# Fewer tokens computed directly: two Strassen groups of 768 tokens take the place of 512 direct tokens and one group of 1024

## Chip, core and metric

One core of one Trainium2 chip. The metric is the device time of one execution in microseconds; lower is better.

## What is computed

```python
# x: (16, 256, 512) f32; cond: (16, 256); W2, weight, rram_variation: (512, 512)
q_emb = relu(cond @ W3 + b3)                         # (16, 512)
h = relu(((256 * x + sum_tokens(x)) * q_emb) @ W2 + b2)
h_q = where(h > 0.33, 0.5, 0)                        # h is never below -0.33
w_q = where(w > 0.2, 0.6, where(w < -0.2, -0.6, 0)) + rram_variation
out = x + einsum('bsd,od->bso', h_q, w_q)
```

There are 4096 tokens (16 batches of 256) of 512 columns. The two big products are the hidden product (tokens by W2, in f32) and the output product (thresholded hidden values by w_q, in f32r with the weight split in a low and a high part).

## The kernel before

Everything lies in SBUF with the features on the partitions: each batch of x is loaded (SP queue), transposed in 32x32 blocks by VectorE (`transpose_batch`, L521 to 534), summed over its tokens (on VectorE for the batches of `VECTOR_SUMS`, by `prepare`, L576 to 583; on ScalarE for the others, by `accumulate`, L433), and scaled in place by ScalarE in four chunks (`scale`, L424 to 431, semaphore `s_xs`).

**Hidden product.** The first 1024 tokens (batches 0 to 3) are multiplied directly: 4 row blocks by 4 column blocks of 128 (L1003 to 1023), and VectorE thresholds the eight banks (`quantize`, L585 to 589). The other 3072 tokens are three groups of 1024. A group is one level of Strassen (Winograd's form): its first half of 512 tokens against its second half, 7 products `p1` to `p7` for each of two output blocks j, each product 2 matmuls of 512 columns; an f32 matmul shows as 2 instructions in the trace, so a product is 4 instructions and a group 56. VectorE makes four token sums for a group (`token_sum_1` to `_4`, L591 to 620, f32, both inputs in SBUF), and for each j it evicts with `c11`, `sum_16`, `sum_167`, `c22`, `c21`, `c12` (L623 to 665). ScalarE copies p1 (`copy_p1`, L452). POOL makes the sums of W2 (`s_mix`) once.

**Output product.** The 8 tiles of 128 tokens that were computed directly are projected directly (`project`, 8 matmuls of 512 columns each) into the banks out_ps; VectorE adds the residual (`finish`, L667). The tiles of the groups are projected in pairs, again by Strassen (`project_pair`, 28 matmuls of 256 columns for two tiles), with hidden sums by POOL and the last pair of tiles done directly. The weight's path: VectorE compares (L748, L750), POOL subtracts and adds rram (L322, L327, 4 instructions each), VectorE transposes (`transpose_weight`, L726), ScalarE rounds to the high part (L479), POOL subtracts the low part (L331). `project(0)` waits for the second low part (`s_wlo`).

**Order.** Each engine's order is written out by hand (VectorE L732 to 824, ScalarE L460 to 518, POOL L306 to 414, TensorE L1003 to 1072, SP L249 to 294). On TensorE: direct products, the 14 products of group 1 with `project(0..3)` put before the last one (L1037 to 1042), `project(4..7)`, then group 2, the four pairs of group 1, group 3, the four pairs of group 2 and the last pairs. The residual tiles lie in the eight slots of x_res: SP loads 8 tiles at once after the weight has been transposed, which lies in the same buffer before (L276 to 284), and loads the next 8 when the stores of the first 8 have landed.

Of the kernel before, what the change touches and what calls it, by code (L numbers as in the profile page):

```python
# [5 lines left out]
def adaln_ffn_kernel(  # L6
# [71 lines left out]
    GROUPS = B // 4  # L78
    LAST = GROUPS - 1

    PAIRS_OF = (0, 4, 4, 3)
# [4 lines left out]
    VECTOR_SUMS = (2, 3, 6, 7)  # L86

    XS_DONE = tuple((n + 1) * KD for n in range(B))
# [3 lines left out]
    with ctx:  # L92
# [34 lines left out]
        th_col = sbuf("th_col", [P, KD])  # L127
        warm = sbuf("warm", [P, D], mybir.dt.bfloat16)
# [10 lines left out]
        res = (x_res, x_res, x_res, x_res_last)  # L139
# [15 lines left out]
        s_x_res = [sem(f"x_res_loaded{g}") for g in range(GROUPS)]  # L155
        s_stored = [sem(f"stored{g}") for g in range(GROUPS)]
# [22 lines left out]
        s_th = sem("threshold_ready")  # L179
        s_mix_done = sem("weight_sum_ready")  # L180
# [47 lines left out]
        def _(sp):  # L228
# [4 lines left out]
            def load_res(g):  # L233
                sp.dma_start(res[g][:], x_tiles[:, g * TILES:(g + 1) * TILES]).then_inc(s_x_res[g], DMA)

            def store(g, tiles):
                for n, c in enumerate(tiles):
                    sp.wait_ge(s_out, (TILES if g == LAST else 0) + n + 1)
                    sp.dma_start(out_tiles[g * TILES + c], res[g][:, c]).then_inc(s_stored[g], DMA)

            def store_pairs(g):
                for c in range(PAIRS_OF[g]):
                    u = 4 * (g - 1) + c
                    sp.wait_ge(s_r12, u + 1)
                    sp.dma_start(out_tiles[g * TILES + c], res[g][:, c]).then_inc(s_stored[g], DMA)
                    sp.wait_ge(s_r2, 2 * (u + 1))
                    sp.dma_start(out_tiles[g * TILES + 4 + c], res[g][:, 4 + c]).then_inc(s_stored[g], DMA)
# [34 lines left out]
            store(0, range(TILES))  # L282
            sp.wait_ge(s_stored[0], DMA * TILES)
            load_res(1)
            sp.wait_ge(s_tr, B - 1)
            load_res(3)
            store_pairs(1)
            sp.wait_ge(s_stored[1], DMA * TILES)
            load_res(2)
            store_pairs(2)  # L290
            store_pairs(3)
            store(3, (3,))
            sp.wait_ge(s_stored[2], DMA * TILES)
            sp.wait_ge(s_stored[LAST], DMA * (TILES + 1))

        @block.gpsimd
        def _(pool):
# [50 lines left out]
            def hidden_sums(g):  # L348
                h = hid[:, g % 2].bitcast(F32)
                a11, a12, a21, a22 = h[:, 0:2, 0:TOK], h[:, 2:4, 0:TOK], h[:, 0:2, TOK:], h[:, 2:4, TOK:]  # L350
                sums = a_sum[:].bitcast(F32)
# [4 lines left out]
                if g > 1:  # L356

                    pool.wait_ge(s_pp[7], 4 * (g - 1))
                nc.gpsimd.tensor_tensor(a_sum[:, 0], a21, a22, ALU.add).then_inc(s_asum, 1)  # L359
                pool.wait_ge(s_asum, 4 * (g - 1) + 1)  # L360
                nc.gpsimd.tensor_tensor(a_sum[:, 1], sums[:, 0], a11, ALU.subtract).then_inc(s_asum, 1)
                nc.gpsimd.tensor_tensor(a_sum[:, 2], a11, a21, ALU.subtract).then_inc(s_asum, 1)
                pool.wait_ge(s_asum, 4 * (g - 1) + 2)
                nc.gpsimd.tensor_tensor(a_sum[:, 3], a12, sums[:, 1], ALU.subtract).then_inc(s_asum, 1)

            def add_pieces(g, c):
                u = 4 * (g - 1) + c
# [7 lines left out]
                for cols in COLS:  # L375
                    nc.gpsimd.tensor_tensor(res[g][:, 4 + c, cols], res[g][:, 4 + c, cols], pieces[:, 2, u % 2],  # L376
                                            ALU.add).then_inc(s_r2, 1)

            def last_hidden_sums(c):

                h = hid[:, LAST % 2].bitcast(F32)
                first, second = slice(c * P, (c + 1) * P), slice(TOK + c * P, TOK + (c + 1) * P)
                a11, a12, a21, a22 = h[:, 0:2, first], h[:, 2:4, first], h[:, 0:2, second], h[:, 2:4, second]
                sums = a_sum[:].bitcast(F32)
                done = 4 * (LAST - 1 + c)
                if c == 0:
# [710 lines left out]
```

## Time and profile before

| | |
|---|---|
| median of 3 runs | 173.6 us (173.01 to 173.63) |
| the profiled execution | 172.84 us, its span 170.9 us |
| TensorE, VectorE, ScalarE, POOL busy | 165.6, 131.4, 67.4, 85.4 us |
| granted TensorE clock | 1.000 (all 40 slices at 9) |
| data moved | 28.99 MB, mean 170 GB/s |

The profiled execution is 0.76 us below the median. 1.94 us of it lie outside the span. A row of the timeline gives start, duration, engine, line, operation and what was written from what; consecutive instructions of an engine overlap by some tens of ns, so the distance between two starts is less than the duration. A row of the chain gives the start and the length of a piece of the chain of work that ended last.

### The profile page before, as it was taken

The numbers are of one execution on the slowest core, as the hardware profiler recorded it, in microseconds if no ns is written. First come the engines' busy times: TensorE is split into PE (matmuls) and PEld (weight loads), VectorE is DVE, ScalarE is ACT, GpSimd is POOL, SyncE is SP. The second block draws the span as 40 slices with busy tenths as digits, with TensorE's granted clock in tenths as the row PEclk, the third lists the DMA queues.
The fourth block names the chain that finished last, engine by engine and source line by source line (L and its number), as shares of the span: only waits on it lengthen the run. The fifth ranks groups of instructions, "written<-read, shape, count | busy, mean of one in ns | idle before, by whom it ended". The sixth has DMA issues, their size and how long they took to land.

```text
span 170.9 us, 2183 instructions
## 1 busy us (share of the span) xinstructions
PE 165.6 (97%) x684; PEld 122.1 (71%) x684; DVE 131.4 (77%) x196; ACT 67.4 (39%) x173; POOL 85.4 (50%) x85
## 2 busy tenths in 40 slices
PE   7989999999999999999999999999999999999991
PEld 2889987777554578686653459997653559999991
DVE  3589998998998999774968998778736267776751
ACT  2155269936102259999007996432000001001000
POOL 3001950849105592560089302759099203999990
PEclk9999999999999999999999999999999999999999
DMA  5999999999600494729949005983293000353166
GB/s 164 255 245 234 228 214 227 222 216 219 121 0 0 118 358 120 140 64 260 398 120 372 16 0 154 342 308 124 94 341 117 0 4 6 118 195 117 70 251 232
DMA packets 31211, 28.99 MB, mean 170 GB/s; under 512 B 1600, under 2 KB 22368, under 8 KB 31200
## 3 DMA queue, kind: packets, MB, share of 16 engines
q1 hardware_dynamic: 30128, 28.07, 60.4%
q10 hardware_dynamic: 1008, 0.79, 1.5%
q8 instruction: 5, 0.08, 0.2%
q14 instruction: 6, 0.05, 0.1%
q0 software_dynamic: 64, 0.00, 0.0%
HBM read 20.47 MB, written 8.39 MB: 169 GB/s over the span
## 4 chain that ended last, share of the span: by engine, by line
PE 87%; DVE 4%; issue 2%; ACT 0%; DVEq 0%; ACTq 0%
PE out_ps L957 12%; PE hid_ps L957 10%; PE out_ps L934 9%; PE out_ps L1020 8%; PE hid_ps L866 6%; PE hid_ps L859 6%; PE hid_ps L927 6%; PE hid_ps L908 5%; PE hid_ps L920 5%; PE hid_ps L883 5%; PE hid_ps L900 5%; PE hid_ps L1007 5%; PE hid_ps L1012 4%; PE hid_ps L934 2%; DVE xT L532 1%
## 5 line engine op out<-in xcount | busy, mean ns | idle before, releaser
L430 ACT ACTIVATE xT<-xT,coef,q_scale 128x256 f32<-128x256 f32 x64 | 33.9, 592 | 13.2 <-DVE coef L583 7.3
L532 DVE STREAM_TRANSPOSE xT<-x_in 128x1024 f32<-128x1024 f32 x15 | 30.7, 2053 | 0.0
L436 ACT ACTIVATE junk<-xT,q_emb 128x256 bf16<-128x256 f32 x40 | 19.8, 496 | 13.5 <-DVE xT L532 13.4
L370 POOL TENSOR_TENSOR x_res<-x_res,pieces 128x256 f32<-128x256 f32 x8 | 5.9, 734 | 24.2 <-DVE x_res L706 24.2
L486 ACT ACTIVATE pieces<-out_ps 128x256 f32<-128x256 f32 x6 | 2.3, 383 | 31.8 <-PE out_ps L957 29.8
L1020 PE MATMUL out_ps<-xT,w_sb 128*128 128x512 f32 x32 | 14.1, 599 | 0.0
L376 POOL TENSOR_TENSOR x_res<-x_res,pieces 128x256 f32<-128x256 f32 x16 | 13.4, 862 | 0.0
L934 PE MATMUL out_ps<-wT_lo,hid 128*128 128x512 f32 x32 | 13.3, 415 | 0.0
L1020 PEld LDWEIGHTS out_ps<-xT,w_sb 128*128 128x128 f32 x32 | 9.8, 309 | 3.8 <-ACT xT L430 0.2
L934 PE MATMUL out_ps<-wT_hi,hid 128*128 128x512 f32 x32 | 12.5, 390 | 0.0
L359 POOL TENSOR_TENSOR a_sum<-hid 128x1024 fp32r<-128x1024 f32 x2 | 4.7, 2348 | 14.6 <-DVE t_sum L611 14.6
L927 PE MATMUL hid_ps<-xT,s_mix 128*128 128x512 f32 x24 | 11.8, 614 | 0.1
L920 PE MATMUL hid_ps<-t_sum,w_sb 128*128 128x512 f32 x24 | 11.3, 592 | 0.0
L908 PE MATMUL hid_ps<-t_sum,s_mix 128*128 128x512 f32 x24 | 11.3, 592 | 0.0
L883 PE MATMUL hid_ps<-t_sum,s_mix 128*128 128x512 f32 x24 | 11.3, 592 | 0.0
L900 PE MATMUL hid_ps<-t_sum,s_mix 128*128 128x512 f32 x24 | 11.3, 592 | 0.0
L866 PE MATMUL hid_ps<-xT,w_sb 128*128 128x512 f32 x24 | 11.0, 601 | 0.0
L859 PE MATMUL hid_ps<-xT,w_sb 128*128 128x512 f32 x24 | 10.9, 597 | 0.0
L331 POOL TENSOR_TENSOR wT_lo<-wT,wT_hi 128x1024 fp32r<-128x1024 f32 x2 | 4.7, 2366 | 11.9 <-ACT wT_hi L479 11.9
L920 PEld LDWEIGHTS hid_ps<-t_sum,w_sb 128*128 128x128 f32 x24 | 7.4, 308 | 3.6 <-issue 1.4
L866 PEld LDWEIGHTS hid_ps<-xT,w_sb 128*128 128x128 f32 x24 | 7.3, 309 | 3.3 <-ACT e L458 0.6
L643 DVE SCALAR_TENSOR_TENSOR e<-hid_ps,th_col,e 128x512 f32<-128x512 f32 x6 | 4.4, 740 | 6.7 <-PE hid_ps L908 6.7
(134 smaller groups left out, 410.6 us busy)
## 6 DMA issues: line engine op xcount, KB each, us to landing
x_in<-in_x SPq DMA_DIRECT2D x24, 256.0 KB, 5.6
x_res<-in_x SPq DMA_DIRECT2D x3, 2048.0 KB, 9.2
out<-x_res SPq DMA_DIRECT2D x24, 256.0 KB, 3.5
x_in<-in_x SPq DMA_DIRECT2D x1, 2048.0 KB, 9.4
out<-x_in SPq DMA_DIRECT2D x7, 256.0 KB, 2.1
x_in<-in_x SPq DMA_DIRECT2D x12, 128.0 KB, 6.2
w_sb<-in_L_cond_W SPq DMA_DIRECT2D x4, 256.0 KB, 6.0
x_res<-in_L_ffn_weight SPq DMA_DIRECT2D x4, 256.0 KB, 7.1
```

The costliest lines, as they stand in the source:

```text
L430: nc.scalar.activation(part, part, ACT.Identity, bias=coef[:, n, k:k + 1], scale=q_scale[:, n, k:k + 1]).then_inc(s_xs, 1)
L532: nc.vector.transpose(xT[:, s, :, cols].rearrange("p j (n t) -> p n j t", t=BLK), x_in[:, p % SLOTS, b * NB:(b + 1) * NB].rearrange("p n ( ...
L859: mm = nc.tensor.matmul(hid_ps[j][:], weight_block(0, 0, j, k), xT[:, g % 2, k, 0:TOK], start=(k == 0), stop=(k == 1))
L866: mm = nc.tensor.matmul(hid_ps[j][:], weight_block(0, 1, j, k), xT[:, g % 2, 2 + k, 0:TOK], start=False, stop=(k == 1), skip_group_check=True)
L883: mm = nc.tensor.matmul(hid_ps[2 - j][:], s_mix[:, 1, j, k], t_sum[:, 1, k], start=(k == 0), stop=(k == 1))
L900: mm = nc.tensor.matmul(hid_ps[3 - j][:], s_mix[:, 0, j, k], t_sum[:, 0, k], start=(k == 0), stop=(k == 1))
L908: mm = nc.tensor.matmul(hid_ps[2 - j][:], s_mix[:, 2, j, k], t_sum[:, 2, k], start=False, stop=(k == 1), skip_group_check=True)
L920: mm = nc.tensor.matmul(hid_ps[0][:], weight_block(1, 1, j, k), t_sum[:, 3, k], start=(k == 0), stop=(k == 1))
L927: mm = nc.tensor.matmul(hid_ps[3 - j][:], s_mix[:, 3, j, k], xT[:, g % 2, 2 + k, TOK:], start=False, stop=(k == 1), skip_group_check=True)
L934: mm = nc.tensor.matmul(bank[:, cols], hid[:, g % 2, k, c * P:(c + 1) * P], w[:, k, cols], start=(k == 0 and w is wT_lo), stop=(k == KD - ...
L957: mm = nc.tensor.matmul(pair_ps[bank][u % 2], hidden[:, k, tokens], w[:, k], start=(start and k == 0 and i == 0), stop=(stop and k == 1 an ...
L1020: mm = nc.tensor.matmul(out_ps[m][:], chunk_columns(w2_sb[:, k], m), xT[:, 0, k, TOK:], start=(k == 0), stop=(k == KD - 1))
```

## The change

- Direct: 512 tokens instead of 1024. Four groups: 768 tokens (batches 2 to 4), 768 (batches 5 to 7), 1024 and 1024. In the 768 groups a half is 384 tokens, so every matmul, eviction and token sum of theirs is 384 or 2x384 wide. xT and hid become rings of 2048 tokens; the same batches lie where they did.
- The four direct banks are thresholded by ScalarE, Sign and then Relu, instead of eight on VectorE. A column of biases (`bias_col`) is added on VectorE.
- Batch 4 is summed by VectorE (`prepare`), batch 6 by ScalarE; before it was the other way round.
- The hidden values of group 1 (tiles 4 to 9) are projected directly too, so that there are ten direct tiles and ten pairs in place of eight and eleven (`PAIRS_OF`). The pair's banks are taken by a written table (`SIDE`, `AHEAD`) as their number is odd.
- Group 1 uses the banks out_ps, group 2 the banks hid_ps.
- Tiles 8 and 9 use slots 0 and 1 of x_res: SP stores tiles 0 and 1, waits for them to land, and loads the residual of 8 and 9 (0.5 MB); the six tiles of group 2 are loaded after tiles 2 to 7 have landed.
- VectorE's two comparisons of the weight stand behind group 1's first evictions, `w_gt` after `c11(1, 1)` and `w_in` after `transpose_batch(6)`.

```diff
-    PAIRS_OF = (0, 4, 4, 3)
+    FIRST = (0, 512, 1280, 2048, 3072)
+    SIZE = (512, 768, 768, 1024, 1024)
+    HALVES = tuple(n // 2 for n in SIZE)
+    LAST_BATCH = tuple((f + n) // N - 1 for f, n in zip(FIRST, SIZE))
+    HALF_BATCH = tuple((f + n // 2 - 1) // N for f, n in zip(FIRST, SIZE))
+    DIRECT = 10
+    PAIRS_OF = {2: 3, 3: 4, 4: 3}
+    SIDE = (0, 1, 0, 0, 1, 0, 1, 0, 1, 0)
+    AHEAD = (None, None, 0, 2, 1, 3, 4, 5, 6, 7)
...
-    VECTOR_SUMS = (2, 3, 6, 7)
+    VECTOR_SUMS = (2, 3, 4, 7)
...
+        def hidden_bank(g, b):
+            return (out_ps if g == 1 else hid_ps)[b][:, 0:HALVES[g]]
...
@@ SP, behind load_pair(7)
-            store(0, range(TILES))
-            sp.wait_ge(s_stored[0], DMA * TILES)
+            store_direct((0, 1))
+            wait_stored(0)
             load_res(1)
+            store_direct(range(2, DIRECT))
+            wait_stored(1)
+            load_res(2)
...
@@ ScalarE
+            def quantize(m):
+                act.wait_ge(s_cls, m + 1)
...
+                nc.scalar.activation(sign[:], hid_ps[m][:], ACT.Sign, bias=bias_col[:, m:m + 1]).then_inc(s_sign, 1)
+                act.wait_ge(s_sign, m + 1)
+                nc.scalar.activation(hid[:, m, 0:TOK], sign[:], ACT.Relu).then_inc(s_cls_hid, 1)
...
             scale_summed(3)
-            sum_and_scale(4)
+            copy_p1(1, 0)
+            copy_p1(1, 1)
+            scale_summed(4)
             sum_and_scale(5)
-            scale_summed(6)
-            copy_p1(1, 0)
-            act.wait_ge(s_coef, len(VECTOR_SUMS))
-            scale(7, (0, 1))
-            copy_p1(1, 1)
-            scale(7, (2, 3))
+            for m in range(KD):
+                quantize(m)
+            sum_and_scale(6)
+            copy_p1(2, 0)
+            copy_p1(2, 1)
+            scale_summed(7)
...
@@ VectorE
             def token_sum_1(g):
+                dve.wait_ge(s_xs, KD * LAST_BATCH[g] + 2)
...
             def finish(c):
-                dve.wait_ge(s_x_res[0], DMA)
+                dve.wait_ge(s_x_res[0 if c < TILES else 1], DMA)
...
             prepare(3)
-            transpose_batch(4)
+            prepare(4)
             transpose_batch(5)
+            token_sum_1(1)
+            token_sum_2(1)
+            dve.wait_ge(s_th, 2)
+            c11(1, 0)
+            token_sum_4(1)
+            token_sum_3(1)
+            sum_16(1, 0)
+            c11(1, 1)
             dve.wait_ge(s_w, QUADS * DMA)
             nc.vector.tensor_scalar(w_gt, ...)
+            sum_167(1, 0)
+            c22(1, 0)
+            c21(1, 0)
+            sum_16(1, 1)
+            transpose_batch(6)
             dve.wait_ge(s_wq, 1)
             nc.vector.tensor_scalar(w_in, ...)
-            for m in range(KD):
-                quantize(0, m)
-            prepare(6)
+            sum_167(1, 1)
+            c22(1, 1)
+            c21(1, 1)
             prepare(7)
-            quantize(1, 0)
...
+            c12(1, 0)
+            c12(1, 1)
+            token_sum_1(2)
+            c11(2, 0)
+            token_sum_2(2)
+            token_sum_4(2)
+            c11(2, 1)
+            token_sum_3(2)
+            sum_16(2, 0)
+            transpose_weight(0)
+            sum_167(2, 0)
+            c22(2, 0)
+            c21(2, 0)
+            transpose_weight(1)
+            sum_16(2, 1)
+            c12(2, 0)
+            transpose_batch(8)
+            sum_167(2, 1)
+            c22(2, 1)
+            c21(2, 1)
             transpose_batch(9)
             finish(0)
             finish(1)
             finish(2)
             transpose_batch(10)
             finish(3)
-            c12(1, 1)
+            c12(2, 1)
             finish(4)
             transpose_batch(11)
-            for c in range(5, TILES):
+            for c in range(5, DIRECT):
                 finish(c)
...
@@ TensorE
+            products(1)
+            p3(1, 1)
+            products(2)
+            for t in range(4):
+                project(t)
+            p3(2, 1)
+            for t in range(4, DIRECT):
+                project(t)
+            for g in (3, 4):
+                products(g)
                 p3(g, 1)
-                for c in range(4):
+                for c in range(PAIRS_OF[g - 1]):
                     project_pair(g - 1, c)
```

`products(g)` is the old order p1 p1 p2 p2 p5 p6 p4 p7 p6 p3 p5 p7 p4. Group 1's `p1` waits for batch 2 and two chunks of batch 3, `p5` for `token_sum_1(1)`, which waits for two chunks of batch 4.

## Rows read from the trace of the kernel before

**Rows 1.** Busy time of each engine, share of the span, instructions (the page).

```profile
PE 165.6 (97%) x684; PEld 122.1 (71%) x684; DVE 131.4 (77%) x196; ACT 67.4 (39%) x173; POOL 85.4 (50%) x85
```

**Rows 2.** The chain that ended last, in order of time: start us, us, what.

```profile
17.01 7.47 PE hid_ps L1012 x32
24.47 14.03 PE out_ps L1020 x32
...
61.01 7.27 PE out_ps L934 x32
68.27 1.72 PE hid_ps L927 x4
...
77.30 3.43 PE hid_ps L859 x8
...
105.50 3.36 PE hid_ps L957 x28
```

**Rows 3.** Timeline of VectorE: start us, us, engine, line, operation, out<-in.

```profile
20.06 2.09 DVE L532 STREAM_TRANSPOSE xT<-x_in 128x1024 f32<-128x1024 f32 x1
...
23.61 4.02 DVE L532 STREAM_TRANSPOSE xT<-x_in 128x1024 f32<-128x1024 f32 x2
...
29.45 1.23 DVE L750 TENSOR_SCALAR x_res<-x_res 128x2048 f32<-128x2048 f32 x1
...
44.90 1.21 DVE L604 TENSOR_TENSOR t_sum<-xT,t_sum 128x1024 f32<-128x1024 f32 x1
46.14 1.23 DVE L619 TENSOR_TENSOR t_sum<-xT,t_sum 128x1024 f32<-128x1024 f32 x1
...
49.08 0.75 DVE L637 SCALAR_TENSOR_TENSOR n<-hid_ps,th_col,e 128x512 f32<-128x512 f32 x1
49.74 2.02 DVE L729 STREAM_TRANSPOSE wT<-x_res 128x1024 f32<-128x1024 f32 x1
52.27 0.75 DVE L643 SCALAR_TENSOR_TENSOR e<-hid_ps,th_col,e 128x512 f32<-128x512 f32 x1 [0.51 <-PE hid_ps L908]
53.13 0.69 DVE L650 TENSOR_TENSOR hid<-hid_ps,e 128x512 fp32r<-128x512 f32 x1
53.73 0.68 DVE L657 TENSOR_TENSOR hid<-hid_ps,e 128x512 fp32r<-128x512 f32 x1
```

**Rows 4.** Timeline of ScalarE.

```profile
3.12 1.28 ACT L422 ACT_TABLE_LOAD   x1 [3.12 <-issue]
...
27.84 2.08 ACT L430 ACTIVATE xT<-xT,coef,q_scale 128x256 f32<-128x256 f32 x4
...
31.92 2.08 ACT L430 ACTIVATE xT<-xT,coef,q_scale 128x256 f32<-128x256 f32 x4
...
40.25 0.60 ACT L458 ACTIVATE e<-hid_ps 128x512 f32<-128x512 f32 x1 [1.38 <-PE hid_ps L859]
...
56.40 1.04 ACT L479 CAST wT_hi<-wT 128x1024 fp32r<-128x1024 f32 x1 [3.56 <-DVE wT L729]
```

**Rows 5.** Timeline of POOL.

```profile
38.27 4.96 POOL L327 TENSOR_TENSOR x_res<-x_res 128x512 f32<-128x512 f32 x4 [2.54 <-DMA x_res<-in_L_ffn_rram_variation]
...
57.52 2.36 POOL L331 TENSOR_TENSOR wT_lo<-wT,wT_hi 128x1024 fp32r<-128x1024 f32 x1 [2.24 <-ACT wT_hi L479]
```

**Rows 6.** Timeline of VectorE around 41 us.

```profile
40.02 0.77 DVE L583 TENSOR_TENSOR coef<-x_sum,q_emb 128x4 f32<-128x4 f32 x1
...
41.95 2.37 DVE L596 TENSOR_TENSOR t_sum<-xT 128x1024 f32<-128x1024 f32 x1 [0.50 <-ACT xT L430]
```

**Rows 7.** SP's load of the last pair of batches; landing of L239's stores from 77.3.

```profile
74.62 2.63 SPq L231 DMA_DIRECT2D x_in<-in_x  x4
...
DMA to landing us min/median/max: 4.6/4.7/4.8
```

**Rows 8.** DMA issues by kind, KB each, median us to landing (the page).

```profile
x_res<-in_x SPq DMA_DIRECT2D x3, 2048.0 KB, 9.2
...
out<-x_in SPq DMA_DIRECT2D x7, 256.0 KB, 2.1
```

More of the change, by code:

```diff
@@ L154, in adaln_ffn_kernel @@
         s_x_in = [sem(f"x_in_loaded{p}") for p in range(PAIRS)]
-        s_x_res = [sem(f"x_res_loaded{g}") for g in range(GROUPS)]
-        s_stored = [sem(f"stored{g}") for g in range(GROUPS)]
+        RES_TILES = ((0, 8), (8, 10), (10, 16), (16, 24), (24, 32))
+        s_x_res = [sem(f"x_res_loaded{i}") for i in range(len(RES_TILES))]
+        STORES = ((0, 2), (2, 8), (8, 10), (10, 16), (16, 24), (24, 32))
+        s_stored = [sem(f"stored{i}") for i in range(len(STORES))]
         s_cond = sem("cond_loaded")
@@ L231, in load_pair, with load_res, store, store_direct @@
                     sp.dma_start(x_in[q * BLK:(q + 1) * BLK, p % SLOTS], x_split[p, q]).then_inc(s_x_in[p], DMA)
[L233 to L239, printed above, removed]
+            def load_res(i):
+                first, end = RES_TILES[i]
+                place = x_res_last if first >= 24 else x_res
+                sp.dma_start(place[:, first % TILES:first % TILES + end - first], x_tiles[:, first:end]
+                             ).then_inc(s_x_res[i], DMA)
+            def store(t):
+                n = [first <= t < end for first, end in STORES].index(True)
+                sp.dma_start(out_tiles[t], res(t)).then_inc(s_stored[n], DMA)
+            def store_direct(tiles):
+                for t in tiles:
+                    sp.wait_ge(s_out, t + 1)
+                    store(t)
+            def wait_stored(n):
+                first, end = STORES[n]
+                sp.wait_ge(s_stored[n], DMA * (end - first))
             def store_pairs(g):
                 for c in range(PAIRS_OF[g]):
-                    u = 4 * (g - 1) + c
+                    u = FIRST_PAIR[g] + c
                     sp.wait_ge(s_r12, u + 1)
-                    sp.dma_start(out_tiles[g * TILES + c], res[g][:, c]).then_inc(s_stored[g], DMA)
+                    store(FIRST_TILE[g] + c)
                     sp.wait_ge(s_r2, 2 * (u + 1))
-                    sp.dma_start(out_tiles[g * TILES + 4 + c], res[g][:, 4 + c]).then_inc(s_stored[g], DMA)
+                    store(FIRST_TILE[g] + HALVES[g] // P + c)
             sp.dma_start(cond_in[:], cond_rows).then_inc(s_cond, DMA)
@@ L769, in _ @@
             c21(1, 0)
-            transpose_weight(1)
             sum_16(1, 1)
-            for m in range(1, KD):
-                quantize(1, m)
-            c12(1, 0)
-            transpose_batch(8)
+            transpose_batch(6)
+            dve.wait_ge(s_wq, 1)
+            nc.vector.tensor_scalar(w_in, w_in, -TH_W, SC_W, ALU.is_lt, ALU.mult).then_inc(s_wq, 1)
             sum_167(1, 1)
@@ L803, in _ @@
                 if g < LAST:
[L804 removed]
+                    transpose_batch(13)
                 c21(g, 0)
@@ L962, in project_pair @@
             def project_pair(g, c):
-                u = 4 * (g - 1) + c
-                first, second = slice(c * P, (c + 1) * P), slice(TOK + c * P, TOK + (c + 1) * P)
-                summed = 4 * (g - 1 + (c if g == LAST else 0))
-                h = hid[:, g % 2]
+                u = FIRST_PAIR[g] + c
+                tile = FIRST_TILE[g] + c
+                first, second = tile_columns(tile), tile_columns(tile + HALVES[g] // P)
+                of_sum = slice(c * P, (c + 1) * P)
+                summed = 4 * (g - 2 + (c if g == LAST else 0))
+                h = hid[:]
                 top, bottom = slice(0, 2), slice(2, 4)
```

431 lines of the change are left out of this document (202 added, 229 removed).

## The prediction

> **What bounds the kernel now.** I read the busy line first. TensorE is busy 165.6 us, 97% of the span, VectorE 77% [rows 1]. Then the chain of waits in order of time: from 9 us on it is TensorE almost alone, direct products to 38.5 us, group 1 to 61.0, projections to 77.3, and so on [rows 2]. So TensorE's own work sets the end, and a change that shortens it pays in full, as long as its inputs keep up. Third, the timeline of VectorE: between 12 and 58 us it has almost no pause either [rows 3]. In that stretch there are two engines without slack, and this is where the change is made. I call T0 the moment when TensorE starts the first direct tile's projection, 61.01 us before [rows 2], and work out T0 first, then what follows it.
>
> **TensorE's work.** The 1024-wide group costs 56 instructions; the second direct half shows the price of one, 14.03 / 32 = 0.438 with its pauses, and a product of four instructions takes 1.72, so 0.43 each [rows 2]. Removed: the second half of the direct product, 14.0 us. The group of 1024 becomes 768: 56 instructions of 384 columns at 0.32 (three quarters of 0.43), 18.0 instead of 24.0. Added: a second such group. Up to T0 (one product of the last group stands behind it) TensorE did 61.0 - 24.5 = 36.5 us of work after the first direct half; now it has 108 instructions of 0.32, 34.8 us. That is 1.7 less. A 256-wide f32 instruction costs 7.47 / 32 = 0.233 where half of 0.43 is 0.215, so up to 0.02 of each may not shrink with the columns: 108 x 0.02 = 2 us at worst, nothing at best. I take nothing, as 384 is wide enough to cover the weight load like 512 (no row shows it), and keep 2 as a bound. After T0: the postponed p3 is 0.43 shorter, two more direct tiles cost 7.27 / 4 x 2 = 3.63, and a pair less saves 3.36 [rows 2]. Together -0.2. If TensorE never waited, the change would be worth 1.9 us.
>
> **VectorE's work up to T0.** T0 needs the low part of the second weight half: the second weight transpose, ScalarE's rounding (1.04) and POOL's subtraction (2.36), with the semaphores 3.6 us from the end of that transpose [rows 3 to 5]. VectorE stands at 23.7 us when batch 3 is prepared, as before (23.61, plus the new column of biases). Its list from there to the end of the second weight transpose, by distances between starts [rows 3]: batches 4 and 7 prepared, 23.61 - 20.06 = 3.55 each, 7.1; batches 5 and 6 transposed, 4.0; the weight's two transposes, 4.0; two comparisons of 1.2, 2.4; eight token sums. One of 1024 elements takes 1.24, and a quarter less columns takes off 0.31 at most; I take 0.95, so 7.6. Four c11 and three sum_16: 0.66 at 512 wide, less 0.13 (a quarter of the columns would be 0.16), 3.7. Three times sum_167, c22, c21: 0.86 + 0.60 + 0.60 at 512, 1.66 at 384, 5.0. Two c12, 0.9. The sum is 34.7 us, so the second weight transpose ends at 58.4 at the earliest and T0 is 62.0 at the earliest, where TensorE's own work would allow 59.3. The eight quantize operations that go to ScalarE take 5.4 us off VectorE, but a further group's sums and evictions cost more. So already without a single pause the 1.7 us of TensorE are not gained but turned into waiting, and 1.0 us is lost.
>
> **VectorE's pauses.** I go through the new order. (a) `token_sum_1(1)` waits for two chunks of batch 4. TensorE starts group 1 at about 24.9, as ScalarE scales batch 3 only then; the two copies of p1, 0.5 each (0.60 at 512 wide [rows 4]), stand ahead of batch 4, which is scaled from 28.4; VectorE waits 0.3. (b) sum_167 and c21 wait for TensorE, 0.2. (c) A comparison moves: POOL's eight weight operations start when `w_in` has been compared, before at 29.45 + 1.23 = 30.7 [rows 3], now at 41.6. Four of them take 4.96 [rows 5], so they run to 51.5, and that is when VectorE makes the coefficients of batch 7 and the token sums of group 2. The rows show what that costs: the coefficients of batch 7 took 0.77 for 4 columns, up to the end of one POOL operation, and the token sum that followed took 2.37 instead of 1.22, up to the end of POOL's row and 1.09 more [rows 5, 6]. Both have two inputs in SBUF; evictions from PSUM beside POOL keep their length. I book 0.85 for the coefficients (46.8 to 47.8), 1.2 for `token_sum_1(2)` and 0.4 for `token_sum_2(2)`. Between nothing (they meet gaps) and 3.3 (each meets a whole operation of 1.24) I take 2.45, nearest to the row. (d) `token_sum_1(2)` waits for ScalarE to scale half of batch 7, 0.3. Together 3.2: T0 = 62.0 + 3.2 = 65.2, 4.2 later than before. TensorE stands idle meanwhile ahead of p5(2,0), p3(2,0) and p7(2,1).
>
> **ScalarE.** A summed and scaled batch takes 31.92 - 27.84 = 4.1 [rows 4]. Batch 5 is done at 34.4, then four times Sign and Relu of 512 columns, 1.3 a pair by the 0.60 row, end at 39.7. Batch 6 is transposed at 40.35, so they cost nothing; only 0.7 us of cover is left, and anything beyond that delays p1(2,0). The one function table load in the trace takes 1.28 [rows 4]. By the Trainium skill (ScalarE: Activation LUTs, section "Table sets: the hidden batching unit") cheap functions such as relu, copy and identity are in every set; Sign is not in that list, and a switch costs 2.7 us by that page. By it the sum would hold if Sign is in the loaded set, and be an estimated 2 us larger (2.7 less the cover) if it isn't. No row shows which.
>
> **After T0.** The new residual slots. SP sends the loads of batches 14 and 15 when batch 11 is transposed, before at 74.62, T0 + 13.6 [rows 7]; now T0 + 13.2 as the p3 between is shorter. It takes 2.65, then tiles 0 and 1 are stored, the second 0.5 later, and such a store lands after 4.7 [rows 7]: T0 + 21.0. The load of tiles 8 and 9 follows. 2 MB land in 9.2 and a store of 256 KB in 2.1 [rows 8], so about 1.0 for each further 256 KB and 3.1 for this one: T0 + 24.2; nearest row above: 4.7. `finish(8)` waits for it and VectorE's whole queue behind it: two finishes 1.3, four token sums 4.9, two c11 1.3, sum_16(3,0) 0.75 [rows 3]. p7(3,0) is released at T0 + 32.5. TensorE would come to it at T0 + 19.5 (ten tiles 18.2, p3 1.3) + 7 products of 1.72 = T0 + 31.5. Loss 1.0, and 0.15 for the weight load that can't run ahead: 1.2, between 0 (the load lands a microsecond sooner) and 2.8. Groups 3 and 4 and their pairs are as before. POOL's hidden sums and pieces are the same per pair, and smaller in group 2.
>
> **The sum.** +4.2 (T0) - 0.2 + 1.2 = +5.2 on the profiled 172.84, so 178.0; the median of the runs stands 0.76 above that execution, so 178.8.
>
> **Rivals.**
> 1. The same place, less of it: POOL and VectorE meet in gaps and the residual comes in time. For it: POOL leaves a gap between operations into which the coefficients slipped. Then T0 = 62.7 to 63.4 and the result is 175.1 to 177.0.
> 2. TensorE stays the only bound: -1.9, 171.7 us, faster. It is one mechanism: the weight's second transpose would have to end at 55.7, 2.7 us ahead of VectorE's list, so the 384-wide operations and sums (28 of them) would have to be 0.1 us cheaper each than I take them, and no lock-out may occur. For it: TensorE's 97%. Against it: the rows give 34.7 us of list for 32 us of time, and before there is hardly any pause in it to use up.
> 3. The bare list: no pauses, residual in time. T0 = 62.0, +1.0 - 0.2, 174.4 us: no difference that can be told from none.
> 4. Something adds to my sum: a table load ahead of Sign (1.28 less 0.7 of cover, +0.6), the 0.02 per instruction, both POOL lock-outs in full: 181 to 184.
>
> **How the numbers follow.** Forecast 0.50 (177.0 to 181.0), rival 1 0.26, rival 2 0.07, rival 3 0.09, rival 4 0.08. A measurement of this kernel tells 0.5%, 0.9 us, from no change. Faster 0.07; same 0.09; slower 0.50 + 0.26 + 0.08 = 0.84. The range of 8 in 10 leaves out rivals 2 and 3 and the upper part of rival 4: 174.8 to 181.2. The point is the forecast's.
>
> **What the profile would show.** Right: a projection of the first direct tile that starts near 65 us; pauses of TensorE between 47 and 65 us released by VectorE; token sums of group 2 longer than 0.95 while POOL adds the weight; POOL's first weight operation near 41.6; VectorE waiting for a DMA ahead of `finish(8)`, and TensorE ahead of p5(3,0) or p7(3,0). Wrong: T0 below 60, no pause of TensorE before it; a table load in front of Sign; instructions of 384 columns at 0.34; a `finish(8)` that doesn't wait.

## The result, and the profile after

| | before | after |
|---|---|---|
| median of 4 runs | 173.47 us (173.01 to 173.63) | 181.39 us (179.14 to 182.11) |
| the profiled execution | 172.84 us, span 170.9 | 179.14 us, span 177.3 |
| ratio after / before | | 1.040 [1.034, 1.046] |

The change makes the kernel 4.0% slower. One of the four runs after, 182.11, fell in the chip's slower state, so the ratio goes by the other three, whose median is 180.97. The forecast was 178.8 us, range 174.8 to 181.2: it holds 180.97, and the median of all four, 181.39, lies 0.2 above its end. The step sum behind it was made against the profiled execution: 178.0, where 179.14 was measured. The median of all four lies 2.25 us above that execution, which was the fastest of them (0.76 before); the forecast had carried the 0.76 over.

The page of the kernel after: busy times, then TensorE, VectorE and the granted clock in 40 slices, then the shares of the chain that ended last.

```profile
PE 166.8 (94%) x696; PEld 124.5 (70%) x696; DVE 132.1 (75%) x201; ACT 73.0 (41%) x182; POOL 81.8 (46%) x82
...
PE   7989989999969999999979999999999999999991
...
DVE  3599998999999994983049999969663447777751
...
PEclk9999999999999999999999999999999999999999
...
PE 52%; DVE 26%; issue 5%; DMA 5%; ACT 2%; SPq 1%; POOL 1%; DVEq 0%
```

TensorE's share of the span fell from 97% [rows 1] to 94% at a full clock, and the chain, TensorE almost alone from 9 us on before [rows 2], now runs through VectorE and a DMA. Where it leaves TensorE is read from the chain itself. In the kernel after, L924 is `p1`, L642 the coefficients, L648 and L657 token sums 1 and 2, L785 the weight transpose, L999 a direct projection, L973 `p7`, L1025 a pair.

```profile
25.34 2.97 PE out_ps L924 x8
...
47.03 1.07 DVE coef L642
...
49.25 2.10 DVE t_sum L648
...
51.80 1.50 DVE t_sum L657
...
59.75 2.06 DVE wT L785
61.83 1.05 ACT wT_hi L542
...
62.95 2.39 POOL wT_lo L377
...
65.48 7.54 PE out_ps L999 x32
...
81.73 5.15 DMA out<-x_res
86.89 3.97 DMA x_res<-in_x
...
99.06 1.97 PE hid_ps L973 x4
...
111.83 3.44 PE out_ps L1025 x28
```

Two places, as foreseen. First, T0 (the first direct projection) is at 65.48 instead of 61.01 [rows 2], behind VectorE's coefficients, token sums and weight transpose. Second, the store of tiles 0 and 1 and the residual load behind it end the wait of group 3. The timeline of VectorE shows the same stretch with its pauses (start, us, line, operation; in brackets the idle time before it and what ended it):

```profile
24.08 2.04 DVE L593 STREAM_TRANSPOSE xT<-x_in 128x1024 f32<-128x1024 f32 x1
...
29.85 0.96 DVE L648 TENSOR_TENSOR t_sum<-xT 128x768 f32<-128x768 f32 x1 [0.31 <-ACT xT L480]
...
49.25 2.10 DVE L648 TENSOR_TENSOR t_sum<-xT 128x768 f32<-128x768 f32 x1 [0.23 <-ACT xT L480]
...
51.80 1.49 DVE L657 TENSOR_TENSOR t_sum<-xT,t_sum 128x768 f32<-128x768 f32 x1
...
59.75 2.05 DVE L785 STREAM_TRANSPOSE wT<-x_res 128x1024 f32<-128x1024 f32 x1
...
90.89 1.29 DVE L722 SCALAR_TENSOR_TENSOR x_res<-out_ps,x_res 128x512 f32<-128x512 f32 x2 [8.48 <-DMA x_res<-in_x]
```

The same token sum takes 0.96 at 29.85 and 2.10 at 49.25. POOL's timeline says what ran beside the second one:

```profile
41.85 4.99 POOL L368 TENSOR_TENSOR x_res<-wT,x_res 128x512 f32<-128x512 f32 x4 [17.71 <-DVE x_res L820]
46.80 5.67 POOL L373 TENSOR_TENSOR x_res<-x_res 128x512 f32<-128x512 f32 x4
```

ScalarE's Sign and Relu, one pair of the four, and what follows the last; no table load stands there:

```profile
34.79 0.67 ACT L517 ACTIVATE sign<-hid_ps,bias_col 128x512 f32<-128x512 f32 x1
35.49 0.63 ACT L519 ACTIVATE hid<-sign 128x512 fp32r<-128x512 f32 x1
...
40.70 0.51 ACT L486 ACTIVATE junk<-xT,q_emb 128x256 bf16<-128x256 f32 x1 [0.25 <-DVE xT L593]
```

And SP's queue around the residual: eight issues of the last two pairs of batches, two stores, the load.

```profile
68.35 12.49 SPq L261 DMA_DIRECT2D x_in<-in_x  x8
80.88 1.28 SPq L271 DMA_DIRECT2D out<-x_res  x2
86.89 0.39 SPq L266 DMA_DIRECT2D x_res<-in_x  x1
```

### The profile page after: what moved, and what is told of

It is laid out like the page before. It is cut to its first block, busy times and chain, and to the rows that moved or that the text cites. A ratio compares the mean times of both kernels' runs of the same rounds, so it can differ in the third digit from the quotient of the medians.

```text
span 177.3 us, 2237 instructions
## 1 busy us (share of the span) xinstructions
PE 166.8 (94%) x696; PEld 124.5 (70%) x696; DVE 132.1 (75%) x201; ACT 73.0 (41%) x182; POOL 81.8 (46%) x82
## 4 chain that ended last, share of the span: by engine, by line
PE 52%; DVE 26%; issue 5%; DMA 5%; ACT 2%; SPq 1%; POOL 1%; DVEq 0%
PE out_ps L1025 11%; PE hid_ps L1025 8%; DVE xT L593 7%; PE out_ps L999 5%; PE hid_ps L992 4%; PE hid_ps L973 3%; DMA out<-x_res 3%; DVE wT L785 2%; DMA x_res<-in_x 2%; PE hid_ps L999 2%; DVE x_sum L640 2%; PE hid_ps L924 2%; PE hid_ps L985 2%; PE hid_ps L949 2%; PE hid_ps L932 2%
## 5 line engine op out<-in xcount | busy, mean ns | idle before, releaser
L722 DVE SCALAR_TENSOR_TENSOR x_res<-out_ps,x_res 128x512 f32<-128x512 f32 x10 | 6.5, 677 | 13.1 <-DMA x_res<-in_x 11.3
L999 PE MATMUL out_ps<-wT_lo,hid 128*128 128x512 f32 x40 | 16.0, 399 | 0.2 <-POOL wT_lo L377 0.2
L999 PE MATMUL out_ps<-wT_hi,hid 128*128 128x512 f32 x40 | 15.6, 390 | 0.0
L410 POOL TENSOR_TENSOR a_sum<-hid 128x768 fp32r<-128x768 f32 (+1 forms) x2 | 4.2, 2086 | 23.2 <-DVE t_sum L663 23.2
L949 PE MATMUL hid_ps<-t_sum,s_mix 128*128 128x512 f32 (+1 forms) x24 | 10.6, 563 | 2.8 <-issue 2.8
L368 POOL TENSOR_TENSOR x_res<-wT,x_res 128x512 f32<-128x512 f32 x4 | 5.0, 1273 | 17.7 <-DVE x_res L820 17.7
L973 PE MATMUL hid_ps<-t_sum,s_mix 128*128 128x512 f32 (+1 forms) x24 | 10.6, 566 | 0.7 <-DVE n L689 0.7
L992 PE MATMUL hid_ps<-xT,s_mix 128*128 128x512 f32 (+1 forms) x24 | 10.9, 578 | 0.2 <-DVE hid L702 0.2
L965 PE MATMUL hid_ps<-t_sum,s_mix 128*128 128x512 f32 (+1 forms) x24 | 10.5, 561 | 0.4 <-DVE t_sum L657 0.4
L985 PE MATMUL hid_ps<-t_sum,w_sb 128*128 128x512 f32 (+1 forms) x24 | 10.4, 557 | 0.0
L924 PE MATMUL hid_ps<-xT,w_sb 128*128 128x512 f32 (+1 forms) x24 | 10.0, 561 | 0.0
L949 PEld LDWEIGHTS hid_ps<-t_sum,s_mix 128*128 128x128 f32 x24 | 4.4, 190 | 8.0 <-issue 7.1
L932 PE MATMUL hid_ps<-xT,w_sb 128*128 128x512 f32 (+1 forms) x24 | 9.9, 557 | 0.0
L999 PEld LDWEIGHTS out_ps<-wT_lo,hid 128*128 128x128 f32 x40 | 7.5, 188 | 2.3 <-issue 0.7
L1025 PE MATMUL out_ps<-b_hi,a_sum 128*128 128x256 f32 x36 | 9.1, 283 | 0.0
```

The source lines that it names most:

```text
L924: mm = nc.tensor.matmul(hidden_bank(g, j), weight_block(0, 0, j, k), xT[:, k, half(g, 0)], start=(k == 0), stop=(k == 1))
L932: mm = nc.tensor.matmul(hidden_bank(g, j), weight_block(0, 1, j, k), xT[:, 2 + k, half(g, 0)], start=False, stop=(k == 1), skip_group_chec ...
L949: mm = nc.tensor.matmul(hidden_bank(g, 3 - j), s_mix[:, 0, j, k], t_sum[:, 0, k, 0:HALVES[g]], start=(k == 0), stop=(k == 1))
L973: mm = nc.tensor.matmul(hidden_bank(g, 2 - j), s_mix[:, 2, j, k], t_sum[:, 2, k, 0:HALVES[g]], start=False, stop=(k == 1), skip_group_chec ...
L985: mm = nc.tensor.matmul(hidden_bank(g, 0), weight_block(1, 1, j, k), t_sum[:, 3, k, 0:HALVES[g]], start=(k == 0), stop=(k == 1))
L992: mm = nc.tensor.matmul(hidden_bank(g, 3 - j), s_mix[:, 3, j, k], xT[:, 2 + k, half(g, 1)], start=False, stop=(k == 1), skip_group_check=True)
```

## The experiments

Two theories stood at the start. Mine: VectorE's list with POOL's lock-outs moves T0, and the residual load behind SP's prefetch costs about two more. The rival: one of the two is only a companion, and taking it away moves the wait elsewhere.

**Residual load ahead of the prefetch** (e1_early_residual).

```diff
-            sp.wait_ge(s_tr, 11)
-            load_pair(7)
             store_direct((0, 1))
             wait_stored(0)
             load_res(1)
+            sp.wait_ge(s_tr, 11)
+            load_pair(7)
```

> The changed kernel with one move on SP: tiles 0 and 1 are stored, awaited and the residual of tiles 8 and 9 loaded ahead of the loads of batches 14 and 15, not behind them. Theory (the residual of tiles 8 and 9 is late): its load is issued near 77 us instead of 86.9 and has landed by 81, finish(8) no longer waits for it, p7(3,0) starts 31.5 us after the first direct projection instead of 33.6, and the whole is 2.1 us shorter than the changed kernel, a profile of 177.0 us. Rival (VectorE reaches the token sums of group 3 late in any case, since ScalarE still scales batches 10 and 11): p5(3,0) starts where it did and the gain is under 0.7 us. Second rival (moving the wait ahead of the loads holds up batch 14): transpose_batch(14) waits for its load and group 3 gets longer.

Measured: 176.86 us (176.71 to 176.94), ratio 1.018 [1.015, 1.021]; profile 176.83. The load is issued at 77.61 instead of 86.89, and the chain has no gap any more from T0 up to group 3:

```profile
65.25 7.52 PE out_ps L999 x32
72.77 1.29 PE hid_ps L992 x4
74.06 10.94 PE out_ps L999 x48
84.99 3.43 PE hid_ps L924 x8
...
91.86 1.72 PE hid_ps L949 x4
```

So the residual step costs 2.3 us in the profiled executions (T0 is 0.23 earlier, so 2.1 of it are the wait). Between the medians it is 4.5, and 3.0 by the second series of the kernel after (after_again below, 179.83), so the median's share isn't settled. The 3.99 that remain over the profile of before are T0 (+4.24) and -0.25 behind it.

**POOL's weight work made thin** (e2_thin_weight: one column in 128, the rest left out), and both edits together (e3_both).

```diff
-    nc.gpsimd.tensor_tensor(w_in[:, quarters[i]], w_gt[:, quarters[i]], w_in[:, quarters[i]],
+    nc.gpsimd.tensor_tensor(w_in[:, quarters[i], 0:1], w_gt[:, quarters[i], 0:1], w_in[:, quarters[i], 0:1],
...
-    nc.gpsimd.tensor_tensor(w_in[:, quarters[i]], w_in[:, quarters[i]], r_in[:, quarters[i]],
+    nc.gpsimd.tensor_tensor(w_in[:, quarters[i], 0:1], w_in[:, quarters[i], 0:1], r_in[:, quarters[i], 0:1],
```

> The changed kernel with POOL's eight weight operations (compare result minus, plus rram) made on one column in 128 only; the rest of the subtraction and of the addition is left out, all else stays. Theory (VectorE's two-input operations wait for POOL's operations in flight): the coefficients of batch 7 take 0.2 instead of 1.06 us, token_sum_1(2) 0.96 instead of 2.10 and token_sum_2(2) 0.96 instead of 1.49, the first direct projection starts 2.3 us sooner, near 63.1 us, and the whole is 2.3 us shorter, 176.8 us. Rival (those waits are covered, as TensorE or ScalarE would be waited for next): the projection starts less than 1 us sooner.

> Both edits, the early residual and POOL's weight operations on one column in 128 (the rest of them left out). Theory: the two losses are independent, 4.4 us shorter than the changed kernel, 174.7 us, and what is left above the kernel before, about 1.5 us, is VectorE's list. Rival (the two overlap: with an earlier projection the other wait grows): under 3.5 us.

Measured: e2 177.94 us (177.04 to 179.70), ratio 1.028 [1.021, 1.034], T0 63.39; e3 175.06 (174.83 to 175.53), ratio 1.008 [1.006, 1.011]. VectorE's timeline of e2:

```profile
46.95 0.16 DVE L642 TENSOR_TENSOR coef<-x_sum,q_emb 128x4 f32<-128x4 f32 x1
...
48.86 0.96 DVE L648 TENSOR_TENSOR t_sum<-xT 128x768 f32<-128x768 f32 x1 [0.81 <-ACT xT L480]
...
50.26 0.95 DVE L657 TENSOR_TENSOR t_sum<-xT,t_sum 128x768 f32<-128x768 f32 x1
```

The three operations shrink from 1.06, 2.10 and 1.49 to 0.16, 0.96 and 0.95, 2.6 us in all, and T0 comes 2.1 sooner, as 0.6 is taken back by a longer wait for ScalarE's scaling (0.81 instead of 0.23). So the lock-outs are shown by taking them away. With both edits the profile is 175.40: 3.7 of the 6.3 us lost are gone, and the ratio falls from 1.040 to 1.008. What is left in e3 is mostly VectorE's list. Its T0 of 63.76 adds up from the start of the list at 24.38 (23.7 in the prediction), 34.6 of list, 1.1 of waits for ScalarE (0.32 and 0.82) and 3.7 of weight work behind it.

**Thresholds back on VectorE** (e4_quantize_vector).

```diff
@@ ScalarE, ahead of sum_and_scale(6)
-            for m in range(KD):
-                quantize(m)
...
@@ VectorE, behind c11(1, 1)
+            for m in range(KD):
+                dve.wait_ge(s_cls, m + 1)
+                nc.vector.tensor_scalar(hid[:, m, 0:TOK], hid_ps[m][:], b2_col[:, m:m + 1], TH_X,
+                                        ALU.add, ALU.is_gt).then_inc(s_cls_hid, 1)
```

> The changed kernel with the four direct banks thresholded on VectorE again, behind c11(1, 1), instead of by Sign and Relu on ScalarE. Theory (VectorE's list sets the start of the first projection): four operations of 0.67 us more in the list, the projection starts 2.7 us later, at 68.2, and the whole is 2.7 us longer, 181.8 us. Rival (TensorE or ScalarE sets it): less than 1 us longer, or shorter, as batch 6 is then scaled sooner.

Measured: 182.10 us (181.75 to 184.45), ratio 1.051 [1.044, 1.058]; the profiled execution is the 184.45 one. Its T0 is 68.95 (68.2 expected). Its second weight transpose starts at 63.21, 3.5 later than in the kernel after, of which 2.6 are the four operations. The rest comes mostly from TensorE, which idled ahead of p3(1, 0) and came back slow, so that VectorE waited 1.67 for its p7. TensorE's timeline, and then the first stretch of the view by windows (busy us and counts of the engines, granted clock, DMA share, GB/s):

```profile
40.62 2.92 PE L994 MATMUL out_ps<-xT,s_mix 128*128 128x384 f32 x4 [2.56 <-DVE hid L700]
```

```profile
35.00:45.00 10.00, 7.44 (x19) 4.03 (x18) 9.46 (x13) 1.81 (x8) 0.36 (x1) 0.83 0.61 124
```

The product behind the pause took 2.92 where the same one takes 1.56 in the kernel after; the granted clock of the stretch was 0.83 (1.00 up to 40 us, 0.66 from 40 to 45). The same happened in group 3, where p5 waits for the late residual load:

```profile
97.64 3.24 PE L951 MATMUL hid_ps<-t_sum,s_mix 128*128 128x512 f32 x4 [2.09 <-issue]
100.67 2.34 PE L967 MATMUL hid_ps<-t_sum,s_mix 128*128 128x512 f32 x4
```

In the kernel after this pause is 1.30 and the two products take 1.96 and 1.88. The residual landed at T0 + 26.2 here and at T0 + 25.4 there, which is the 0.8 that the pause is longer. The granted clock was 0.82 and 0.84 from 95 to 105 us, and 1.9 of the 5.3 us between the two profiles lie behind T0. ScalarE's quantize is the good part of the change.

**Both comparisons together, early** (e5_weight_compared_together): e1, and `w_in` compared directly behind `w_gt`, so that POOL is done before the sums of group 2.

```diff
             nc.vector.tensor_scalar(w_gt, w_in, TH_W, SC_W, ALU.is_gt, ALU.mult).then_inc(s_wq, 1)
+            dve.wait_ge(s_wq, 1)
+            nc.vector.tensor_scalar(w_in, w_in, -TH_W, SC_W, ALU.is_lt, ALU.mult).then_inc(s_wq, 1)
             sum_167(1, 0)
...
             transpose_batch(6)
-            dve.wait_ge(s_wq, 1)
-            nc.vector.tensor_scalar(w_in, w_in, -TH_W, SC_W, ALU.is_lt, ALU.mult).then_inc(s_wq, 1)
```

> The kernel with the early residual (e1), and VectorE's second comparison of the weight directly behind the first, ahead of sum_167(1, 0), where it was behind transpose_batch(6). POOL's weight operations then run from 37.6 to 47.7 instead of 41.6 to 52.5, nothing is left out. Theory (VectorE's token sums wait for POOL): token_sum_1(2) and token_sum_2(2) take 0.96 each, the coefficients of batch 7 still 0.9; the first direct projection starts 1.7 us sooner than in e1, at 63.6, and the whole is 1.7 us shorter, 175.2 us. Rival (only the order matters: TensorE's p7(1,0) and p3(1,0) now come 1.2 us later and are not made up): no gain.

Measured: 176.40 us (176.35 to 176.57), ratio 1.018 [1.017, 1.020]: 0.5 less than e1's median at the same ratio (the kernel before, run beside each, was 0.4 lower too), and T0 at 64.84, only 0.4 sooner. The token sums are short again, but the comparison, moved forward by 1.2, now stands ahead of the result for which p3(1, 0) waits. First VectorE's timeline, then TensorE's:

```profile
43.31 0.62 DVE L695 SCALAR_TENSOR_TENSOR e<-out_ps,th_col,e 128x384 f32<-128x384 f32 x1 [1.23 <-PE out_ps L973]
...
50.31 0.96 DVE L648 TENSOR_TENSOR t_sum<-xT 128x768 f32<-128x768 f32 x1 [0.78 <-ACT xT L480]
```

```profile
39.13 1.56 PE L992 MATMUL out_ps<-xT,s_mix 128*128 128x384 f32 x4 [1.18 <-DVE hid L702]
```

TensorE waits 1.18 for VectorE, so VectorE waits 1.23 for TensorE two products later (p7), and 0.78 for ScalarE. The pause has changed its name. Here the rival is right, or nearly: at most 0.5 was gained where 1.7 was expected.

**Shortening the weight's path and VectorE's list** (e7_low_part_in_chunks: e5, with group 2's `c11` on ScalarE as Sign and Relu, `sum_16(2, 1)` ahead of the second weight transpose, and the second half's rounding and low part in four chunks that `project(0)` takes one by one; e8_p3_first: e7 with p3(2, 1) ahead of the projections, and VectorE's evictions of (2, 1) directly behind the second weight transpose).

```diff
-                nc.scalar.copy(wT_hi[:, :, cols], wT[:, :, cols]).then_inc(s_whi, 1)
+                    for k in range(KD):
+                        nc.scalar.copy(wT_hi[:, k, cols], wT[:, k, cols]).then_inc(s_whi, 1)
...
+                    if t == 0:
+                        pe.wait_ge(s_wlo, k + 2)
...
+            p3(2, 1)                          # e8
             for t in range(4):
                 project(t)
-            p3(2, 1)                          # e8
```

> e5 with three more edits: both c11 of group 2 by Sign and Relu on ScalarE, which is idle from 50 to 58 us; the second half of the weight's high and low part in four chunks, for which the first direct tile waits one by one; and sum_16(2, 1) ahead of the second weight transpose. Theory (the start of the projections hangs on VectorE's list and the 3.6 us of weight work behind it): the list is 1.1 us shorter, the weight work 1.6, so the first projection starts at 61.0 to 61.5 and the whole takes 172.8 to 173.4 us, level with the kernel before. Rival (TensorE's pauses around p5(2,0) and p3(2,0) set it, and c11 on ScalarE comes later than on VectorE, which holds up p4(2,0)): over 174.5 us.

> e7 with p3(2,1), the last product of group 2, ahead of the projections instead of behind the fourth, and VectorE's sum_167, c22 and c21 of (2, 1) directly behind the second weight transpose. Theory: TensorE's pause for the weight, up to 1.3 us, is filled by that product, and the kernel is 0.5 to 1.0 us faster than e7. Rival: the product waits for c22(2,1), which comes 1 us behind the transpose, so the pause only moves: within 0.3 us of e7.

Measured: e7 175.20 us (175.10 to 175.58), ratio 1.012 [1.010, 1.014], T0 62.84; e8 174.84 (174.70 to 175.49), ratio 1.010 [1.007, 1.012]. e7's T0 is 2.0 earlier than e5's, but its profile only 1.1 shorter: the 2 MB residual landed after 10.6 us and held the fifth projection 0.32. From T0 to that projection e7 takes 9.34 us and e5 8.81, and the six tiles behind it take 11.18 instead of 10.94; together that is 0.8 of the 0.9. e7 missed what I expected (172.8 to 173.4) and its rival's "over 174.5" holds. e8 gained 0.4 over e7 (0.5 between the profiles), at or below the lower end of the 0.5 to 1.0 of its theory; it is the best complete version, 1% behind the kernel before.

**The kernel after once more** (after_again), for its spread.

> The changed kernel once more, unchanged. Its profiled execution was 179.1 us and its other runs 181.0 to 182.1; with the early residual this spread is gone (176.7 to 176.9). Theory (the time until the residual loads land varies from execution to execution, 9.2 us for 2 MB in one profile and 11.4 in another, and this kernel alone hangs on it): times again spread by 1 us or more, and a profile above 180 us shows finish(0) or finish(8) released by the DMA 2 us later than in the first. Rival (something else varies, such as TensorE's clock after a pause): such a profile has its loads at the same times and a granted clock below 1 between 85 and 105 us.

Measured: 178.93, 179.50, 180.16 and 183.75 us, ratio 1.038 [1.035, 1.041]. The profile, of the 178.93 run, repeats the first one: the pause ahead of p5(3, 0) is 1.36, the residual step the same. The median is 179.83, 0.90 above it and not 2.25. Neither profile of this kernel is of a long run, but e4's is: it has the same late load, and there a longer pause (2.09) brought the clock down, and two products behind it took 1.7 us more. The clocks of the long runs here fit that (0.990 to 0.991 at 180.97 to 182.11, 0.972 at 183.75, as in e4's), but the 180.16 run had the full clock (1.000) and the 179.50 one 0.987, so the clock can't be all of it, and which of them was which isn't settled.

The spreads say little more. Without the one highest run each of after, after_again and e2, the four kernels with the late residual load spread by 1.2 to 2.7 us (after and e4 2.7, after_again and e2 1.2), with those three runs by 2.7 to 4.8. Those with the early one spread by 0.2 to 1.0 (e1, e3, e5, e7, e8, and e9 without its 331), and e10 by 1.8.

**The comparisons made thin too** (e9_no_comparisons, and again as e9_again for its profile): e8 with VectorE's two comparisons and POOL's eight operations on one column in 128, the rest left out (the first of these edits is shown).

```diff
-            nc.vector.tensor_scalar(w_gt, w_in, TH_W, SC_W, ALU.is_gt, ALU.mult).then_inc(s_wq, 1)
+            nc.vector.tensor_scalar(w_gt[:, :, 0:1], w_in[:, :, 0:1], TH_W, SC_W, ALU.is_gt, ALU.mult).then_inc(s_wq, 1)
...
```

> e8 with VectorE's two comparisons of the weight and POOL's eight weight operations made on one column in 128; the rest of them is left out. Theory (the narrower groups do save TensorE 1.9 us, but VectorE's list is longer than TensorE's up to the projections): with 2.3 us less in the list VectorE's pause for p7(1, 1) and TensorE's for c22(1, 0) go too; the projections start 1.5 to 2.5 us sooner than in e8 and the kernel takes 172.4 to 173.2 us, at or below the kernel before. Rival (the saving of the narrower groups does not exist, or TensorE's start at 25 us and ScalarE's scaling of batches 4 and 7 are the limit): 174 us or more.

> e9 once more, for a profile of an undisturbed execution (the comparisons and POOL's weight operations on one column in 128, the rest left out): 173.8 us, level with the kernel before. Theory (behind VectorE's list the chain from group 1's last evictions over batch 7 to token_sum_1(2) is the next limit): TensorE waits at p5(2,0) and p3(1,0) for 1 us or less each, and the projections start 0.5 to 1.5 us behind TensorE's own 60.6 (24.9 to the start of group 1, 27 products of 1.29, and pauses of 0.3 at p5(1,0)). Rival (something behind the projections costs more than before): the projections start at TensorE's own time and the rest of the kernel is longer than the 106.4 - 0.2 us that it took before.

Measured: 173.81 us in ten runs, nine of them from 173.39 to 174.39 (the tenth took 331), ratio 1.002 [0.999, 1.005]; then 173.86 in eight (173.54 to 174.19), ratio 1.002 [1.000, 1.005]. With 2.1 us of VectorE's work and nearly all of POOL's eight operations left out, the kernel is level with the one before, not faster. The chain of e9_again's profile shows why. L989 is p7, L713 and L720 the evictions `sum_167` and `c22`, L1008 is p3:

```profile
53.87 1.30 PE hid_ps L989 x4
...
55.20 0.63 DVE e L713
...
55.92 0.57 DVE hid L720
...
56.53 1.56 PE hid_ps L1008 x4
58.09 1.29 PE hid_ps L965 x4
```

From the end of p7 to the start of p3 the two evictions with their semaphores take 1.36 us; one product of 384 columns lies between (p6, 1.29) and no longer covers them. p3 comes 0.07 late, finds an empty engine and takes 1.56 instead of 1.29: the three products take 58.09 - 53.87 = 4.22 instead of 3.87, 0.35 lost at each of four p3. Before, with 512 columns, the product between took as long as the evictions, 1.72, and p3 lost 0.19 (this row of its chain):

```profile
53.95 1.91 PE hid_ps L927 x4
```

All the small losses from 25.13 to 63.60, where group 1, group 2 and the last p3 are done, come to 38.47 - 112 x 0.3225 = 2.35 us, and group 1 starts 0.66 later than the work behind the first direct half did before (25.13 against 24.47). These 3.0 outweigh the 1.9 of TensorE's work that the change saves. The profile is 0.7 longer than before's, so 0.4 come back; 0.3 of it in group 3, which takes 24.60 us from its first product to the first pair (81.79 to 106.39) and took 24.86 before.

**Comparisons on POOL** (e10_comparisons_pool): e8 with both comparisons as POOL's `tensor_scalar`, in quarters.

```diff
+            pool.wait_ge(s_tsum, 4)
+            for i in range(4):
+                nc.gpsimd.tensor_scalar(w_gt[:, quarters[i]], w_in[:, quarters[i]], TH_W, SC_W,
+                                        ALU.is_gt, ALU.mult).then_inc(s_wq, 1)
+            for i in range(4):
+                pool.wait_ge(s_wq, i + 1)
+                nc.gpsimd.tensor_scalar(w_in[:, quarters[i]], w_in[:, quarters[i]], -TH_W, SC_W,
+                                        ALU.is_lt, ALU.mult).then_inc(s_wq, 1)
...
```

> e8 with the two comparisons of the weight on POOL, in quarters, behind token_sum_3(1), and nothing left out. POOL is idle from 24 us on. Theory: VectorE's list is 2.3 us shorter as in e9; POOL's sixteen operations run from 34 to 49 us if a compared quarter takes 0.65 us, so they meet the coefficients of batch 7 (1 us of waiting) but not the token sums of group 2; 173.0 to 174.0 us. Rival (POOL's comparison is as slow as its two-input operations, 1.25 us a quarter): POOL runs to 54 us, locks the token sums of group 2 and holds up the weight's transposes, 175 us or more.

Measured: 181.95 us (180.92 to 182.71), ratio 1.048 [1.043, 1.053]. POOL's timeline, then VectorE's:

```profile
34.59 7.93 POOL L369 TENSOR_SCALAR wT<-x_res 128x512 f32<-128x512 f32 x4 [10.17 <-DVE t_sum L689]
42.61 7.93 POOL L373 TENSOR_SCALAR x_res<-x_res 128x512 f32<-128x512 f32 x4
50.62 6.86 POOL L377 TENSOR_TENSOR x_res<-wT,x_res 128x512 f32<-128x512 f32 x4
```

```profile
49.19 0.96 DVE L674 TENSOR_TENSOR t_sum<-xT 128x768 f32<-128x768 f32 x1 [0.79 <-ACT xT L495]
50.29 0.96 DVE L683 TENSOR_TENSOR t_sum<-xT,t_sum 128x768 f32<-128x768 f32 x1
51.35 1.84 DVE L697 TENSOR_TENSOR t_sum<-xT,t_sum 128x768 f32<-128x768 f32 x1
...
59.95 2.02 DVE L811 STREAM_TRANSPOSE wT<-x_res 128x1024 f32<-128x1024 f32 x1 [4.29 <-POOL x_res L382]
```

A comparison takes POOL 2.0 us a quarter where VectorE does the whole weight in 1.2 [rows 3]. POOL ends at 62.4 and the first weight transpose waits 4.29 for it. TensorE then idled 4.57 ahead of a p3 and came back slow (2.23 and 2.51 for two products, at a granted clock of 0.89 and 0.77 in the stretches 60 to 65 and 65 to 70 us). The theory that POOL has room for it fell.

## Why the prediction was right, and which term was too small

| step of the sum | predicted | measured |
|---|---|---|
| T0 | 65.2 (+4.2) | 65.48 (+4.47) |
| VectorE's list up to the second weight transpose | 34.7 | 34.6 |
| POOL's lock-outs | 0.85 + 1.2 + 0.4 = 2.45 | 0.90 + 1.14 + 0.53 = 2.57 |
| waits for ScalarE | 0.3 and 0.3 | 0.31 and 0.23 |
| after T0, without the residual | -0.2 | -0.25 (e1) |
| residual load of tiles 8 and 9 | +1.2 | +2.1 |
| profiled execution | 178.0 | 179.14 |
| median over it | +0.76 | +2.25; +0.90 in after_again |

- **The signs named.** T0 near 65, POOL's first weight operation near 41.6 (41.85), long token sums beside it, and a `finish(8)` that waits for a DMA all stand in the profile.
- **What bounds.** Right. The list is 61.80 (end of the transpose) - 24.08 - 2.57 - 0.54 = 34.6. It starts 0.4 later than the 23.7 of the sum, which is most of what T0 is late by. TensorE's saving was real, 1.29 for a product of 384 columns instead of 1.72 [rows 2], three quarters exactly, and it went into waits. The 0.02 per instruction that I kept as a bound doesn't exist.
- **Lock-outs.** Right in place and size, and e2 shows them by taking them away. The 0.2 booked for `sum_167` and `c21` doesn't show as a wait of its own, so two small misses (this and the later start) cancel in part. By the Trainium skill (SBUF — State Buffer, section "Who interferes with whom") a VectorE instruction with two SBUF inputs contends with a GpSimd instruction that reads SBUF, while one with at most one SBUF input does not (outside the modes that use both port pairs). The trace agrees: the long ones have two inputs in SBUF, and the eviction from PSUM between the two slow sums kept its 0.60 us.
- **ScalarE.** Right: 34.79 to 40.45, and ScalarE then still waits 0.25 for the transpose. By the Trainium skill's list (ScalarE: Activation LUTs, "Table sets: the hidden batching unit"), which doesn't name Sign, a switch was possible; the trace shows none.
- **The residual step was under-sized.** The sum had 1.2 and e1 shows 2.1. I let the load land at T0 + 24.2; it landed at T0 + 25.4. The two stores took 1.28 to issue and 5.15 to land (4.7 assumed), and 512 KB took 3.97 where I took 3.1, out of a rate worked from 2 MB. p7(3, 0) was released at T0 + 33.6, not 32.5. My upper bound of 2.8 held it.
- **The median.** This was the larger miss in the first series: 2.25 above the profile instead of 0.76. In after_again it is 0.90, so part of the 2.25 is the luck of which of four runs was profiled, the fastest. With the early load it is gone (e1: median and profile 0.03 apart). e4's profile shows one way a late load lengthens a run, through a longer pause and the clock behind it; no long run of the kernel after itself was profiled.
- **Rivals.** Number 3, the bare list, 174.4: e3 leaves the list and the waits for ScalarE and measured 175.06. Number 2, TensorE alone at 171.7, wasn't reached even by e9; its case left out the late p3 of a 384-wide group and the later start of group 1, which no row given with the prediction shows. Number 1 fell because both of its conditions did: the sums met POOL, and the residual was late.

## What to carry to other kernels

A saving on the busiest engine is worth only the slack of the second engine in that very stretch: add up the second engine's list first, with what it loses to a neighbour, before counting the saving. Narrower tiles also shorten the cover: when one product is shorter than the chain of evictions that the next but one waits for, each such place loses the difference and the slower product behind the pause (0.07 and 0.27 us here). And a load that has to wait for stores goes into its queue ahead of prefetches that nobody awaits yet; that one move was worth 2.3 us here between the profiled executions.

## What the hardware did that I had not expected

- POOL's one-input `tensor_scalar` of 128x512 takes 2.0 us (7.93 for four), longer than its two-input `tensor_tensor` of the same size at 1.24 (4.96 for four [rows 5]).
- That one-input instruction didn't hold up VectorE's two-input ones, nor they it: in e10 the coefficients took 0.16 at 47.30 and the sum 0.96 at 49.19, and the four POOL instructions of that row 1.92 each. The first sum that began behind POOL's two-input ones (from 50.62) took 1.84. The section of the Trainium skill named above (SBUF — State Buffer, "Who interferes with whom") speaks of a GpSimd instruction that reads SBUF, whatever its inputs; here the measurement decides.
- A pause of TensorE of 2.56 us in e4 was followed by a product at half rate (2.92 for 1.56), at a granted clock of 0.66 from 40 to 45 us: part of these 5 us at 1.2 GHz, the rest at 2.4. One of 2.09 in e4 and one of 4.57 in e10 did the same. The pauses of up to 1.5 us between products in the kernel after left its clock at 0.999 over the profiled execution.
- The first 2 MB residual load takes 9.1 to 9.4 us in the profiles of before, after, after_again, e2 and e10, 9.6 to 10.0 in e8, e9_again and e4, 10.6 in e7 and 11.4 in e1, e3 and e5, with no change to the load itself. Why isn't shown.
